# A gated recurrence of 256 steps in which four semaphore waits stand at other instructions

## What is computed

```
def cell(h, x):
    gi = x @ W_ih + b_ih
    gh = h @ W_hh + b_hh
    i_r, i_z, i_n = jnp.split(gi, 3, axis=-1)
    h_r, h_z, h_n = jnp.split(gh, 3, axis=-1)
    r = jax.nn.sigmoid(i_r + h_r)
    z = jax.nn.sigmoid(i_z + h_z)
    n = jnp.tanh(i_n + r * h_n)
    h_new = (1.0 - z) * n + z * h
    return (h_new, h_new)
_, hs = jax.lax.scan(cell, initial_state, xs)     # 256 steps, h is 8 x 512
x = x + swapaxes(hs, 0, 1)
```

## Time and profile before

| what | value |
|---|---|
| median of 3 runs | 2088.25 us (2083.18 to 2089.26) |
| the profiled execution, its own time | 2086.28 us |
| its span, first to last instruction | 2084.4 us |
| busy: PE, DVE, ACT, POOL | 1862.4, 1268.6, 1117.4, 376.8 us (89%, 61%, 54%, 18%) |
| granted TensorE clock, mean | 0.878 |

### The profile page before, as it was taken

The page is one execution under the profiler, slowest core; times in us unless marked ns, Lnnn a source line. Parts: engine busy times, 40 slices in busy tenths (PEclk is TensorE's granted clock), DMA queues, the critical chain, the costliest instruction groups (busy, mean ns, idle before and its releaser), DMA issues. The chain is left out here.

```text
span 2084.4 us, 86393 instructions
## 1 busy us (share of the span) xinstructions
PE 1862.4 (89%) x32542; PEld 1372.1 (66%) x32542; DVE 1268.6 (61%) x5543; ACT 1117.4 (54%) x4105; POOL 376.8 (18%) x1398
## 2 busy tenths in 40 slices
PE   7877998999989999999978998989898999999876
PEld 4234364454635546355557898989898989889775
DVE  6454483645736366374143777777777777777766
ACT  0342636546364463636553565656565666666554
POOL 3000000000000000000000333333334333333335
PEclk7788999999999999999998697969697988989556
DMA  5122203132041321302123000000000000000002
GB/s 190 70 66 71 68 21 106 53 76 83 9 110 42 82 78 35 95 15 74 69 61 107 1 1 0 0 0 0 0 0 0 0 0 0 0 0 0 0 0 81
DMA packets 103527, 86.76 MB, mean 42 GB/s; under 512 B 15616, under 2 KB 90496, under 8 KB 103440
## 3 DMA queue, kind: packets, MB, share of 16 engines
q1 hardware_dynamic: 101392, 84.38, 14.0%
q10 hardware_dynamic: 1664, 1.18, 0.2%
q0 software_dynamic: 384, 0.01, 0.0%
HBM read 60.20 MB, written 21.00 MB: 39 GB/s over the span
## 5 line engine op out<-in xcount | busy, mean ns | idle before, releaser
L1257 PE MATMUL bank_pair_A<-moving,rep 128*128 128x16 f16 x8192 | 328.4, 172 | 67.2 <-DVE moving L1497 64.1
L1257 PEld LDWEIGHTS bank_pair_A<-moving,rep 128*128 128x128 f16 x8192 | 268.4, 99 | 96.4 <-DVE moving L1497 81.2
L1257 PE MATMUL bank_pair_B<-moving,rep 128*128 128x16 f16 x8192 | 321.3, 171 | 0.0
L1257 PE MATMUL bank_pair_C<-moving,rep 128*128 128x16 f16 x8192 | 321.3, 171 | 0.0
L1356 ACT ACTIVATE r_gate<-r_pre 128x16 f32<-128x16 f32 x512 | 110.5, 216 | 305.6 <-DVE r_pre L1447 305.6
L1257 PEld LDWEIGHTS bank_pair_C<-moving,rep 128*128 128x128 f16 x8192 | 265.8, 99 | 0.0
L1257 PEld LDWEIGHTS bank_pair_B<-moving,rep 128*128 128x128 f16 x8192 | 265.8, 99 | 0.0
L1244 PE MATMUL bank_pair_D<-x_part,w_in 128*128 128x256 f16 x1536 | 211.5, 286 | 5.8 <-ACT gi_rz L1383 3.3
L1137 POOL TENSOR_TENSOR x<-x,w_in 128x512 f32<-128x512 f32 x8 | 10.2, 1274 | 962.5 <-DMA w_in<-w_in 962.5
L1447 DVE TENSOR_REDUCE r_pre<-bank_pair_A 128x16 f32<-128x32 f32 x512 | 98.1, 192 | 137.5 <-PE bank_pair_A L1257 136.4
L834 ACT ACTIVATE probs<-bank_pair_A 128x1024 f32<-128x1024 f32 x128 | 131.0, 1024 | 90.5 <-PE bank_pair_A L598 90.1
(11 more groups left out here) (260 smaller groups left out, 3639.4 us busy)
## 6 DMA issues: line engine op xcount, KB each, us to landing
rep<-parts SPq DMA_DIRECT2D x256, 64.0 KB
parts<-parts SPq DMA_DIRECT2D x48, 256.0 KB, 2.1
q_rep<-parts SPq DMA_DIRECT2D x32, 256.0 KB, 4.7
k_rep<-parts SPq DMA_DIRECT2D x64, 128.0 KB, 2.8
w_in<-in_x_dram SPq DMA_DIRECT2D x8, 512.0 KB, 4.0
x<-in_x_dram SPq DMA_DIRECT2D x8, 512.0 KB, 4.3
parts<-parts SPq DMA_DIRECT2D x32, 128.0 KB, 2.5
out_dram<-res SPq DMA_DIRECT2D x16, 256.0 KB, 2.1
```

The lines of the kernel that those rows point to most:

```text
L1257: last = nc.tensor.matmul(ps[part][:, o:o + 2 * B], w[:, k, (first + c) * P:(first + c) * P + P], moving[j % 2][:, k, :, :].rearrange("p s ...
```

## The change

Four waits of a step are placed differently; no operation is added, taken away or reordered.

- DVE waited for n_in at `sum_n(0)`. Now PE waits for it, ahead of R1 with K_B, whose sum `sum_r(1)` reads.
- DVE waited for x_add at `sum_z(0)`. Now it waits at the write of `state` in `new_state(0)`.
- At `moved`, the wait for zh_ok (the difference) stands ahead of that for z_ok (the gate z of part 1); before it was the other way round.

```
                 gate(pN, N_, 0, K_B).then_inc(n_ps, 1)
+                pe.wait_ge(n_in, step + 1)
                 gate(pR, R, 1, K_B).then_inc(r_ps, 1)
...
                 def sum_n(part):
-                    if part == 0:
-                        dve.wait_ge(n_in, step + 1)
                     dve.wait_ge(n_mul, step * 2 + (part + 1))
...
                 def moved():
+                    dve.wait_ge(zh_ok, step * 2 + 2)
                     dve.wait_ge(z_ok, step * 2 + 2)
-                    dve.wait_ge(zh_ok, step * 2 + 2)
                     nc.vector.tensor_tensor(z_new[:, SLICE[1], :], z_gate[:, SLICE[1], :], z_old[:, SLICE[1], :], ALU.mult).then_inc(zn_ok, 1)
...
-                    for out, done in ((following[:, SLICE[part], 0, :], hi_done), (new[:, SLICE[part], :], st_ok)):
-                        nc.vector.scalar_tensor_tensor(out=out, in0=of[:, SLICE[part], :], scalar=scale, in1=to[:, SLICE[part], :],
-                                                       op0=ALU.mult, op1=ALU.add).then_inc(done, 1)
+                    nc.vector.scalar_tensor_tensor(out=following[:, SLICE[part], 0, :], in0=of[:, SLICE[part], :], scalar=scale,
+                                                   in1=to[:, SLICE[part], :], op0=ALU.mult, op1=ALU.add).then_inc(hi_done, 1)
+                    if part == 0:
+                        dve.wait_ge(x_add, step + 1)
+                    nc.vector.scalar_tensor_tensor(out=new[:, SLICE[part], :], in0=of[:, SLICE[part], :], scalar=scale,
+                                                   in1=to[:, SLICE[part], :], op0=ALU.mult, op1=ALU.add).then_inc(st_ok, 1)
...
                 sum_r(0)
-                dve.wait_ge(x_add, step + 1)
                 sum_z(0)
```

## The result

The changed kernel takes 2095.83 us, median of 18 runs (2087.17 to 2102.54); the kernel before takes 2087.73 us beside it, median of 18 (2080.91 to 2094.75). The ratio is 1.0037, 95% interval 1.0025 to 1.0049: slower by 0.37%, some 8 us. The forecast was 2098, slower, +10.6 by the sum over the steps.

What follows compares the result with a forecast made beforehand. PE and DVE hand each other one chain through 256 steps. Terms of -0.6, +2.3 and +8.9 us gave +10.6 us, 2096.9 on the profiled time, 2098.9 on the median; 2098 was taken, range 2088 to 2108.

Steps and rivals of the forecast that it cites:

- The exchange in moved: At moved on DVE: the gate's wait now pays 0.10 us, the difference's 0.03, so moved starts 0.05 later in product steps.
- The register step ahead of `state`: On DVE between `moving` and `state`: the x_add wait's register instruction costs 0.01 us a step, from 0 to 0.03.
- sum_z(0) and sum_n(0): On DVE: each loses its wait ahead and starts about 0.07 us earlier, hidden by n_terms of part 1 or unneeded: 0.
- the steps j = 0 without a product: 42 steps, 15 in the last block: the difference comes later there, so -0.025 and +0.01 us each, -0.6 us together.
- PE's wait: On PE ahead of R1, for n_in: +0.045 us in 22 steps, from 0.02 to 0.07; nothing where already met.
- the late copy: 22 steps (26, 28, 30 of blocks 0 to 6, last block's first): POOL's copy ends after R1's old start; +2.3 us together.
- The steps at the lower clock: 15 steps at the head of product stretches, where PE's matmuls take 0.84 us more and PE has no gap: 0.
- the exchange costs nothing: Rival at moved: two waits are met together, their order is no matter; only 1 us is lost, 2088.3 us. Chance 0.13.
- the difference is the late one: Rival at moved: the gate ends early, so moved gains 0.07 us in 213 steps, -15 us, 2072 us. Chance 0.09.
- PE stumbles at each step: Rival at R1: its weight load can't be taken ahead, up to 0.05 us in 241 steps, +12 us, 2110. Chance 0.05.
- The share of the clock: Rival on PE: from 7 to 21 lower-clock steps move the time by -7 to +5 us; counted in the spread, no chance given.
- PE's gap ahead of R1: Sign for the profile after: in steps 26, 28 and 30 PE has this gap and POOL is named as its releaser.

Runs made afterwards that it cites:

- swap: The kernel before with only moved's two waits exchanged, zh_ok ahead of z_ok: 2098.10 us against 2088.94, ratio 1.0042.
- unswap: The changed kernel with moved's two waits put back as before, the other edits kept: 2086.19 us, ratio 0.9982 to the kernel before.
- pewait: The kernel before with only the n_in wait moved from DVE's sum_n(0) to PE ahead of R1: 2082.31 us, ratio 0.9961.
- xadd: The kernel before with only the x_add wait moved from sum_z(0) to the write of state: 2081.18 us, ratio 0.9962.

## Why the prediction came out

**The exchange in moved, +0.05 a step: right, and a little small.** It is 0.058 in product steps, and swap and unswap show it by itself from both sides. The gate ends 0.055 behind the difference, and z_new went from 0.104 behind the difference's end (2.096 to 2.200) to 0.102 behind the gate's (2.154 to 2.256).

**The register step ahead of `state`, +0.01 a step: wrong, it is 0.** `state` is 0.082 behind `moving` in both kernels, and unswap is 3.334. In the records the register instruction is over at 1.564 us into the step, `moving` runs from 1.553 to 1.718. Of +0.06 forecast, 0.05 and 0.01, the first was worth 0.058 and the second nothing: the sum held by chance. The rule that the prediction quotes from the Trainium skill (VectorE: DVE Perf Modes, "The DRAIN you can't avoid") gave this 0 too, but its reason doesn't hold here: `state` still starts 0.08 into a `moving` of 0.165. The same paragraph goes on that a next operation that is not held starts earlier, which the prediction left out and the trace agrees with.

**sum_z(0) and sum_n(0), 0: right for the changed kernel, wrong without the exchange.** pewait and unswap are 0.06 shorter in the steps j = 0 without a product: n_terms of part 1 hides n0's lead from `moving`, but not from n1 and the difference, which the prediction passed over. In the changed kernel this lead is worth nothing. There the wait that stands ahead is the gate's, and it sets the start of moved, with n0's lead (3.413) or without it (swap, 3.413). In the last block z_old and moved in such a step (DVE) and its gate (ACT), the answers to the earlier trace rows:

```profile
1935.51 0.17 DVE L1479 SCALAR_TENSOR_TENSOR z_old<-cand,state 128x16 f32<-128x16 f32 x1
1935.84 0.18 DVE L1485 TENSOR_TENSOR z_new<-z_gate,z_old 128x16 f32<-128x16 f32 x1 [0.15 <-ACT z_gate L1357]
```

```profile
1935.52 0.21 ACT L1357 ACTIVATE z_gate<-z_pre 128x16 f32<-128x16 f32 x1
```

The gate ends at 1935.73, the difference at 1935.68, and moved starts 0.11 behind the gate. The forecast, too, took the gate's end and 0.10 for the new start (1989.25, rows 4 and 5) in place of a start that the late difference had given. Its -0.015 (-0.025, and +0.01 for the register step) measured -0.006 and -0.017.

**PE's wait, +0.045 in the steps of the late copy: the wait came as forecast, its price did not, and that +0.105 lies near 0.125 is luck.** R1 starts 0.06 behind the copy (0.05 forecast), r_pre 0.39 behind R1 (as forecast). By itself, in pewait, this makes r_pre of part 1 0.030 later (0.791 in place of 0.761, which DVE's hold-up had set and not PE's sum; I hadn't seen that). In the changed kernel r_pre comes 0.026 earlier, at 0.735: the exchange brings the copy 0.06 nearer to the step's start. The prediction added the exchange and PE's wait, and in these steps they share one stretch of time. What made up for it, 0.083 ahead of `state`, was in no term. The step's +0.125 is 0.058 for the exchange, -0.026 at r_pre, +0.083 at `state`, and 0.01 without a place.

**The steps at the lower clock, 0, with 7 to 21 of them in the spread: right.** There were 13 in place of 15, -1.9 us, 0.93 each (4.26 - 3.33). In this pair of profiles that is most of what lies between +10.6 and +8.4. It says nothing of the medians of 18 runs, which differ by 8.1 as well; how many such steps the other runs had is not on record. By kinds: +0.058 x 98 = 5.7 for steps 9 to 23, +1.2 for 25, 27 and 29, +2.6 for the late copy, +0.3 and +0.4 for steps 24 and 31, +0.8 and -0.3 for the last block's j = 1 and j = 0, -0.1 for the steps j = 0 without a product, -0.3 for the split steps, -0.2 for steps 0 and -1.9 for the clock: +8.2 of 8.4.

**The rivals.** That the exchange costs nothing falls with swap and with the wait's own record. The Trainium skill (Perfetto Trace Analysis, "DVE / Act Engine Instruction") describes one queue in which an instruction waits until all its semaphores are there. The trace agrees for the wait inside (0.03 from signal to start). The other wait is no part of the instruction in the records but an instruction of its own ahead, of which that section doesn't speak. That the difference is the late one falls: the gate was late by 0.055 in product steps, and in the others it came 0.05 behind the difference once n0 had its lead (1935.73 and 1935.68). That PE stumbles at each step falls with pewait: product steps 3.337 against 3.333. The share of the clock was as weighed. One sign named ahead failed: PE's gap ahead of R1 is there, but the profile names no releaser for it, POOL or other.

What stays open: the cause of DVE's hold-ups in steps 24, 26, 28 and 30, and why the ratios of xadd and pewait are lower than their traces explain.

## What to carry to other kernels

Where an instruction has two waits, find out which signal comes last in the steps that count, and let that be the wait inside the instruction; the early one may stand ahead at no price, the late one pays 0.07 us there. Gains and losses of single waits don't add up where their signals share a stretch of time: here n0's lead of 0.06 vanished behind the exchange. Look for the same fault at every instruction of the chain, since the largest gain here (0.8%) lay at one that the change didn't touch. A wait moved to an engine with slack costs nothing while its signal is early, but look through all kinds of steps for those in which it is late.

## What the hardware showed that I had not expected

- A third wait whose signal is long there lengthens the wait instruction ahead from 0.021 to 0.049 us, and the step by 0.034 us, if it joins the late one.
- DVE's own row of instructions has hold-ups of 0.08 to 0.12 us at one place of steps 24, 26, 28 and 30, the steps j = 0 of the loop with the product of N, with everything that it waits for present. Their place and presence change with the code: ahead of r_pre of part 1 in before (0.103; 0.116 in step 24), ahead of `state` in after (0.083; 0.09 in step 24), nearly none in xadd. The late copy is not their cause, since step 24 has them too. That it is the supply of instructions behind a loop's branch is only a guess; no run tests it.
- A register instruction between two operations is free on DVE where the second would start 0.08 us behind the first anyway.
